# A graph kernel on one core: the first normalisation's root moved from ScalarE to GpSimd and VectorE, six tiles of x in flight, a coarser edge search, and a new order of encoder and adjacency steps

## The reference

```python
h = relu(layernorm(x))                      # x: 1250 nodes x 1024
h = sigmoid(h @ wenc.T + benc)              # 1250 x 500
h2 = h @ conv_weight
agg = segment_sum(h2[src] * edge_weight[:, None], dst)    # 20000 edges, sorted by dst
x = x + (agg + h @ lin_weight.T) @ wdec.T + bdec
h = relu(layernorm(x))
h = h @ W.T + b
# with self loops: out[row] = sum over edges of deg[row]**-0.5 * deg[col]**-0.5 * h[col]
x = x + out
```

## Time and profile before

| | us |
|---|---|
| median of three runs | 539.5 |
| the profiled execution's own time | 540.06 |
| span of the profile | 537.9 |
| TensorE multiplies, busy | 493.9 (92%) |
| VectorE busy | 268.1 (50%) |
| ScalarE busy | 182.8 (34%) |
| GpSimd busy | 30.3 (6%) |
| mean granted TensorE clock | 0.978 |

### The profile page before, as it was taken

The page is one execution under the profiler, slowest core; times in us unless marked ns, Lnnn a source line. Parts: engine busy times, 40 slices in busy tenths (PEclk is TensorE's granted clock), DMA queues, the critical chain, the costliest instruction groups (busy, mean ns, idle before and its releaser), DMA issues.

```text
span 537.9 us, 9411 instructions
## 1 busy us (share of the span) xinstructions
PE 493.9 (92%) x3716; PEld 425.6 (79%) x3716; DVE 268.1 (50%) x663; ACT 182.8 (34%) x348; POOL 30.3 (6%) x27
## 2 busy tenths in 40 slices
PE   3468398899999999999999999999999999999997
PEld 3357397799887877878988887888888888888975
DVE  4587587777768488452456778651111111211211
ACT  0753577855445111211433454550120120120110
POOL 1200000000000000000000000011021030030030
PEclk9977799999999999999999999899999999999999
DMA  8302031155411004006443000700100101100102
GB/s 309 98 11 93 25 118 51 57 175 201 136 66 50 12 0 192 0 2 216 186 151 122 0 2 16 299 1 39 40 1 39 41 1 40 40 1 39 40 1 71
DMA packets 16462, 40.11 MB, mean 75 GB/s; under 512 B 1984, under 2 KB 10442, under 8 KB 16034
## 3 DMA queue, kind: packets, MB, share of 16 engines
q1 hardware_dynamic: 16098, 39.09, 20.2%
q0 software_dynamic: 320, 0.39, 0.2%
HBM read 27.95 MB, written 11.52 MB: 73 GB/s over the span
## 4 chain that ended last, share of the span: by engine, by line
PE 86%; ACT 6%; DVE 6%; issue 1%; POOL 0%; ACTq 0%; DVEq 0%; POOLq 0%
PE bank L1043 21%; PE bank L1044 20%; PE bank L1045 20%; PE bank L1059 16%; PE bank L1163 3%; PE bank L1148 2%; ACT h L598 2%; DVE stats L747 1%; PE bank L1253 1%; PE bank L1150 1%; PE bank L1152 1%; DVE we L431 1%; PE bank L1123 1%; DVE before L771 1%; ACT L608 1%
## 5 line engine op out<-in xcount | busy, mean ns | idle before, releaser
L1059 PE MATMUL bank<-a,h_hi 128*128 128x256 f16 (+3 forms) x400 | 87.5, 273 | 0.0
L1059 PE MATMUL bank<-a,h_lo 128*128 128x256 f16 (+3 forms) x400 | 87.4, 272 | 0.0
L1043 PE MATMUL bank<-w_hi,z 128*128 128x512 f32 (+1 forms) x160 | 62.7, 392 | 1.1 <-DVE z L1018 1.1
L1028 DVE SCALAR_TENSOR_TENSOR x<-bank,dis_u,x 128x512 f32<-128x512 f32 (+1 forms) x20 | 14.9, 750 | 95.2 <-PE bank L1045 95.2
L1044 PE MATMUL bank<-w_lo,z 128*128 128x512 f32 (+1 forms) x160 | 62.4, 390 | 0.0
L1045 PE MATMUL bank<-w_hi,z 128*128 128x512 f32 (+1 forms) x160 | 62.3, 389 | 0.0
L718 ACT CAST z<-bank 128x256 fp32r<-128x256 f32 (+1 forms) x40 | 14.4, 371 | 129.3 <-PE bank L1059 129.3
L589 POOL TENSOR_TENSOR x<-x,bt 128x1024 f32<-128x1024 f32 (+1 forms) x10 | 24.0, 2398 | 477.4 <-ACT bt L726 477.4
L1043 PE MATMUL bank<-h0T,we 128*128 128x256 f32 (+3 forms) x160 | 48.0, 300 | 2.1 <-DVE we L431 2.1
L1044 PE MATMUL bank<-h0T,we 128*128 128x256 f32 (+3 forms) x160 | 46.2, 289 | 0.0
L1045 PE MATMUL bank<-h0T,we 128*128 128x256 f32 (+3 forms) x160 | 46.0, 288 | 0.0
(11 more groups left out here) (140 smaller groups left out, 1072.5 us busy)
## 6 DMA issues: line engine op xcount, KB each, us to landing
adj_scratch<-stage SPq DMA_DIRECT2D x50, 125.0 KB, 1.8
raw<-adj_scratch SPq DMA_DIRECT2D x2, 2500.0 KB, 9.3
h<-x SPq DMA_DIRECT2D x9, 512.0 KB, 4.3
x<-x SPq DMA_DIRECT2D x9, 512.0 KB, 5.2
out<-x SPq DMA_DIRECT2D x9, 512.0 KB
w_raw<-w SPq DMA_DIRECT2D x4, 1024.0 KB, 9.1
wd_raw<-wdec SPq DMA_DIRECT2D x1, 2048.0 KB, 7.8
we_raw<-wenc SPq DMA_DIRECT2D x1, 2000.0 KB, 9.5
```

The lines of the kernel that those rows point to most:

```text
L1028: v.scalar_tensor_tensor(xs, bank[banks_of[g]][0:n, :], dis_u[0:n, t:t + 1], xs, ALU.mult, ALU.add).then_inc(bank_free, 1)
L1043: pe.matmul(o, lhs[0], rhs[0], start=first, stop=False, skip_group_check=True)
L1059: ins = pe.matmul(o, h1[i][0:n, k, 128 * f:128 * (f + 1)], moving, start=(k == 0 and part == 0 and i == 0), stop=(k == T - 1 and part == p ...
```

## The change

1. **The root.** `roots` for the first norm becomes `scale`: VectorE adds epsilon, GpSimd raises to the power -0.5 (one TENSOR_TENSOR of 128x2), VectorE makes a Newton step (three instructions) and the bias, for two tiles together. ScalarE does no square root in the first layer. The second norm keeps its root on ScalarE.
2. **Six tiles.** `XRING` is 6, and all six are loaded at the start; the encoder weight arrives in two halves between them, and the encoder bias last.
3. **The search** looks at every sixteenth destination: 10 comparisons and 20 multiplies. `starts` is a step of its own between `stats 0` and `stats 1`. GpSimd clears the two bias rows and fills two more small tiles ahead of the gather.
4. **The order.** `edges` comes after block 1's transposes and after all of block 0's encoder. In blocks 1 to 3, two encoder groups come before the next block's transposes and two after. `swl 0` is four steps with windows between them.
5. **The windows.** The three multiplies of `hot` are one of 750 elements (line 850), and ScalarE makes all four widened copies (660).

```diff
-ALIGN = 8
+ALIGN = 16
-XRING = 4
+XRING = 6
-    steps = statistics(0, 2) + norms(0) + turn(0) + [("lo", *s) for s in turn(0)] + cut_we + statistics(2, 4)
-    dense = encoder(0)[:2] + norms(1) + [("edges",)] + turn(1) + encoder(0)[2:] + statistics(4, 6) + norms(2) + turn(2)
-    dense += mix(encoder(1), statistics(6, 8) + norms(3)) + turn(3) + mix(encoder(2), statistics(8, 10) + norms(4)) + turn(4)
-    dense += [("load", "wc")] + encoder(3) + cut_wc + encoder(4) + [("load", "wl")]
-    dense += [("g", t) for t in range(5)] + mix(cut_wl, [("g", t) for t in range(5, T)])
-
-    cost = {"t": 0.8, "e": 2.5, "g": 2.6}
+    steps = [("stats", 0), ("starts",), ("stats", 1), ("scale", 0, 2)] + norms(0) + turn(0) + [("lo", *s) for s in turn(0)] + cut_we
+    dense = encoder(0)[:2] + statistics(2, 4) + norms(1) + encoder(0)[2:] + turn(1) + [("edges",)]
+    for b in range(1, NB - 1):
+        dense += mix(statistics(2 * b + 2, 2 * b + 4) + norms(b + 1), encoder(b)[:2]) + turn(b + 1)
+        if b == NB - 2:
+            dense += [("load", "wc")]
+        dense += encoder(b)[2:]
+    dense += mix(encoder(NB - 1), cut_wc) + [("load", "wl")]
+    dense += [("g", t) for t in range(5)] + mix(cut_wl, [("g", t) for t in range(5, T)]) + [("swl", 0, f) for f in range(KF)]
+    cost = {"e": 1.1, "g": 2.0, "swl": 1.5}
-    begin = dense.index(("t", 1, KD // 2 - 1)) + 1
+    begin = dense.index(("edges",)) + 1
...
+            nc.gpsimd.memset(hT[0][96:128, KF - 1, :].bitcast(F32), 1.0).then_inc(bias_rows, 1)
+            nc.gpsimd.memset(hT[1][96:128, KF - 1, :].bitcast(F32), 0.0).then_inc(bias_rows, 1)
...
+                if s[0] == "scale":
+                    t0, t1 = s[1:]
+                    pool.wait_ge(var_ready, t0 // 2 + 1)
+                    nc.gpsimd.tensor_tensor(std[:, t0:t1], dis[:, t0:t1], minus_half[:, 0:t1 - t0], ALU.pow).then_inc(power_ready, 1)
...
+                    y, q, var = std[:, t0:t1], dsq[:, t0:t1], dis[:, t0:t1]
+                    v.tensor_scalar(var, mv[:, t0:t1, 1], EPS, None, ALU.add).then_inc(var_ready, 1)
+                    dve.wait_ge(power_ready, t0 // 2 + 1)
+                    link(v.scalar_tensor_tensor(q, y, -0.5, y, ALU.mult, ALU.mult))
+                    link(v.tensor_tensor(q, q, var, ALU.mult))
+                    link(v.scalar_tensor_tensor(rstd[:, t0:t1], q, 1.5, y, ALU.add, ALU.mult))
+                    v.scalar_tensor_tensor(nbias[:, t0:t1], mv[:, t0:t1, 0], -1.0, rstd[:, t0:t1], ALU.mult, ALU.mult).then_inc(rstd_ready, 1)
...
+                    shape = [128, SUB, WPARTS, KC // 2, 2]
+                    v.tensor_tensor(o_key[:, r, :, 1:, :].rearrange("p w n (c i) -> p w n c i", i=2), key.unsqueeze(2).broadcast_to(shape),
+                                    wq[:, ws, :, :].unsqueeze(3).broadcast_to(shape), ALU.mult).then_inc(pair_ready, 1)
```

More of the change, by code:

```diff
@@ L83, in statistics @@
     def statistics(a, b):
-        return [("stats", t) for t in range(a, b)] + [("roots", a, b)]
+        return [("stats", t) for t in range(a, b)] + [("scale", a, b)]
     def norms(b):
@@ L136, in schedule @@
     turned = [("c", t, q) for t in range(T) for q in range(len(QS))]
-    steps += [("swl", 0), ("general",)]
+    steps += [("general",)]
     for n in range(NS):
         if n:
-            steps += [("swl", n)]
+            steps += [("swl", n, f) for f in range(KF)]
         units = [("unit", n, k) for k in range(T)]
@@ L202, in build @@
         if s[0] == "swl":
-            for f in range(KF):
-                bank_for(("s", s[1], f), *dense)
+            bank_for(("s", s[1], s[2]), *dense)
         elif s[0] == "c":
@@ L271, in build @@
         cb = small("cb", [P, T], F32)
+        minus_half = small("minus_half", [P, 2], F32)
         epsc = small("epsc", [P, 1], F32)
@@ L300, in build @@
         we = [at(f"we{i}", [P, KD, F], F32R, R_G + 16000 * i) for i in range(2)]
-        h0 = at("h0", [P, XRING, D], F32, R_X)
+        h0 = [at(f"h0_{i}", [P, D], F32, R_X + 4096 * i if i < 4 else R_G + 32768 + 4096 * (i - 4)) for i in range(XRING)]
         edges = at("edges", [EP, RG, 3, ROW], I32, R_RAW)
@@ L352, in build @@
         x_in = [sem(f"x_in{t}") for t in range(T)]
-        cut_in = {n: sem(f"{n}_in") for n in ("we", "wc", "wl", "wd")}
+        cut_in = {n: sem(f"{n}_in") for n in ("wc", "wl", "wd")}
+        we_in = [sem(f"we_in{i}") for i in range(2)]
         w1_in = [sem(f"w1_in{i}") for i in range(W1_LOADS)]
@@ L592, in _ @@
         def _(act):
+            act.wait_ge(iotas, 11)
             for s in STEPS:
@@ L772, in _ @@
             ins.then_inc(before_ready, 1)
-            dve.wait_ge(starts_acc, 1)
-            link(v.tensor_scalar(start_f[:], wbank[1][0:EP, 2 * ROWS + 2:2 * ROWS + 2 + RG], -1.0, 0.0, ALU.add, ALU.max))
-            v.tensor_copy(start[:], start_f[:]).then_inc(starts_ready, 1)
             for s in STEPS:
@@ L781, in _ @@
                     dve.wait_ge(x_in[t], 16)
-                    statistics(t, h0[0:n, t % XRING, :], t, n)
-                elif s[0] == "norm":
-                    norm(s[1], 0)
+                    statistics(t, h0[t % XRING][0:n, :], t, n)
+                elif s[0] == "starts":
+                    dve.wait_ge(starts_acc, 1)
+                    link(v.tensor_scalar(start_f[:], wbank[1][0:EP, 2 * ROWS + 2:2 * ROWS + 2 + RG], -1.0, 0.0, ALU.add, ALU.max))
+                    v.tensor_copy(start[:], start_f[:]).then_inc(starts_ready, 1)
+                elif s[0] == "scale":
+                    t0, t1 = s[1:]
+                    dve.wait_ge(mv_ready, t1)
+                    y, q, var = std[:, t0:t1], dsq[:, t0:t1], dis[:, t0:t1]
[5 more added lines that the diff above has]
+                    v.scalar_tensor_tensor(nbias[:, t0:t1], mv[:, t0:t1, 0], -1.0, rstd[:, t0:t1], ALU.mult, ALU.mult).then_inc(rstd_ready, 1)
                 elif s[0] == "cut":
@@ L999, in _ @@
                 elif s[0] == "norm1":
-                    norm(s[1], 1)
+                    norm1(s[1])
                 elif s[0] == "h1lo":
```

101 lines of the change are left out of this document (45 added, 56 removed).

## The result

The changed kernel takes **548.2 us** (median of four runs, 546.87 to 549.55) against 539.5 (four runs beside them): the ratio is 1.015, with a 95% interval of 1.0108 to 1.0192. It is slower, and outside the range of the prediction.

The account below looks back on a forecast made before the run. TensorE bounds the kernel, with 38.5 us idle, all in the first 110 us. Idle time +2.8 (41.3 against 38.5) and work -5.0 make -2.2; 540.06-2.2-0.56 gives 537.3 us, range 534.0 to 541.8.

Parts of the forecast that it names:

- Search: Start: halved comparisons and multiplies take 2.2 us of TensorE work and 2.0 us of idle time away.
- I cost them at nothing: Start: GpSimd's two clearings (1.13 us each) beside VectorE's comparisons cost nothing, at most 2.2 us.
- rival D: Start: clearings hold VectorE's comparisons, the search ends 2.2 us later, 539.1 us in all; chance 0.12.
- The norm starts at 13.6: First norm: starts at 13.6 us against 16.99 before, so block 0's transposes start 3.3 us earlier.
- rival C: Blocks 0 and 2 to 4: GpSimd's power is slow, at 2.4 us the kernel takes 543.9 us; chance 0.10.
- The waits: TensorE's idle times up to the first `sk`, listed place by place: 41.3 us in all against 38.5 before.
- the core of the prediction: Gaps of 2 to 3 us ahead of `e 2 0` and `e 3 0`, which the trace before does not have.
- After so short an idle stretch the transposes run at full speed: Block 2's transposes: behind 2.6 us idle they take 2.2 us instead of 3.5, so -1.3 us of work.
- Rival B: `e 0 0` and `e 1 0`: TensorE is not slowed there, -3.2 us more, 534.1 us; chance 0.36.
- Rival E: Late windows: VectorE falls behind as the fused multiply costs 0.2 to 0.3 us more, +5, 542.3 us; chance 0.05.

Follow-up runs that it names:

- Experiment 1: Changed kernel with the two clearings moved behind the gather and the first power: 547.54 us, ratio 1.0132 to the kernel before.
- 7: Old order with the changed parts, first power ahead of the gather, clearings behind both, one-column sigmoid first on ScalarE: 535.96 us, ratio 0.9888.
- 9: Changed kernel with fields as own step, low parts first, last two `swl 0` groups behind windows, start of 7, next block's norms ahead of `e b 1`: 521.0 us.
- Experiment 2: Changed kernel with the old order of steps, old cost table and `swl 0` whole behind the last window: 540.77 us, ratio 1.0001.
- 11: Kernel before the change with filling multiplies in TensorE's waits: 534.72 us, ratio 0.9907.
- experiment 3: Changed kernel with filling multiplies of the identity in TensorE's waits, no wait shortened: 542.74 us, ratio 1.0045 to the kernel before.
- experiment 10: Kernel of 9 with filling multiplies ahead of the transposes of blocks 2 to 4 and the first window: 520.6 us, ratio 0.9628.

## Why the prediction was wrong

Forecast was -2.2 us for the profiled execution and +9.3 came, 11.5 more. By its own steps:

**Search: right.** TensorE's 4.4 us became 2.3. The wait ahead of it was to be 5.2 and is 7.1, which belongs to the next two points.

**"I cost them at nothing" (the clearings): wrong, rival D.** It gave D a chance of 0.12, and cited as support for zero that small steps beside a clearing kept their 0.16 us. The step that failed is that these say nothing of a 128x128 `tensor_scalar`. The clearings held the three identities ahead of the comparisons, not the comparisons as D had it, for 1.8 us. Experiment 1 shows it: with the clearings moved, the comparisons and all behind them up to block 0's transposes came 1.8 us earlier, and nothing else ahead of these moved.

**"The norm starts at 13.6": wrong by 3.1.** 1.8 are the clearings. The gather began 1.07 us behind the start numbers (9.60 + 0.17 to 10.84), not 0.3; experiment 1 has 1.08 with the clearings out of the way, so they are not the reason, and no run shows what is. (With the power ahead of it, in 7 and 9, the gather starts 0.24 us behind the power.) The power took 0.72 us for 0.4 (rival C's far end did not come). The table load stayed, as forecast. The price against the forecast is 3.0 us of idle time (1.9 ahead of the search, 1.1 ahead of block 0).

**The waits: right nearly everywhere.** Forecast and measured: fields 5.2 and 5.47, first window 3.5 and 3.36, block 2's transposes 2.6 and 2.23, `e 2 0` and `e 3 0` 2.7 and 2.80, block 3's and block 4's transposes 2.2 and 2.23, `e 4 0` 1.2 and 1.34, ahead of `sk` 2.5 and 2.59. Only the windows that wait for a copy cost 1.3 and not 0.5. The two new gaps that were called the core of the prediction are there.

**"After so short an idle stretch the transposes run at full speed": wrong, and the largest miss.** The step took one row, block 3's transposes behind 2.53 us, as a rule for all waits of that length, although its own rows had the opposite as well: `e 0 2` at 0.50 behind a wait of 2.60 us. It counted -2.8 us of busy time, +4.5 came, 7.3 us apart. The single terms, from the first multiply of a step to the next step: block 1's transposes did run at full speed (3.67 to 1.91 us, -1.8 for the -1.5 that was counted). Block 2's kept nearly all of their time (3.15 to 3.04, -0.1 for -1.3). Block 3's (1.81 to 3.27), `e 2 0` (2.95 to 4.44) and `e 3 0` (2.92 to 4.40), which the forecast had at full speed without a word, cost 1.5 us each.

Not all of the 4.5 is the clock. With filling, TensorE's own multiplies ahead of the first `sk` take 9.0 us less in the changed kernel (148.2 to 139.3) and 5.6 less in the kernel before (145.8 to 140.2). So 3.3 of the 4.5 is half speed, 6.1 from the forecast. The other 1.2 remain at full speed. They are mostly in the windows: one that stands ahead of a wait is shown with 0.66 us and another with 0.50, and there are more waits.

Rival B leaned on the same rule from the other side ("since only one idle stretch before block 2 is now over 5 us behind dense work") and fell with it. Its price for `e 1 0` was that of `e 0 2`: before, `e 1 0` ran at full speed (2.96 us).

**Rival E fell.** The fused multiply takes less than the three. From one window's operands to the next VectorE needs 1.06 us in after; before it needed 1.20 (44.75 to 45.94), with 0.68 for the three:

```profile
48.87 0.27 DVE L844 TENSOR_TENSOR o_key<-iota_k,kkey 128x250 bf16<-128x250 bf16 x1
49.07 0.47 DVE L846 TENSOR_TENSOR o_src<-iota_s,skey 128x640 bf16<-128x640 bf16 x1
49.47 0.53 DVE L850 TENSOR_TENSOR o_key<-o_key,wq 128x750 bf16<-128x750 bf16 x1
49.93 0.27 DVE L844 TENSOR_TENSOR o_key<-iota_k,kkey 128x250 bf16<-128x250 bf16 x1
```

Together: 3.0 for the start, 6.1 for the clock, 1.2 for the other busy time, 0.8 for the copies, and 0.4 that I can't assign make the 11.5. This is the sum as the forecast wrote it, busy and idle time apart. It is not what the clock costs net: at full speed TensorE comes earlier to the next wait and waits longer there. Net, half speed costs 5.5 us in the change and 6.0 before, nearly the same.

**Why the new order loses at all** is a second question, since the forecast had it even. Experiment 2 puts it at 7.4 us (8.0), 11 at 8.0 (7.5) with the clock held. The traces of 3 and 11 allow a count of everything ahead of the first `sk` that is not the kernel's own TensorE work, with filling multiplies counted as waiting: 40.5 us in the old order, 49.0 in the new one. Block 2's transposes gain 4.9 (9.0 to 4.1), and those of blocks 3 and 4 gain 0.6 together; `e 2 0` and `e 3 0` lose 2.9 each, and what follows block 4's transposes 6.3 (1.34 ahead of `e 4 0`, 2.4 for windows that wait for a copy, one of them 1.47, and 2.59 ahead of `sk`), where before there was nothing. With the fields and the first window (-0.1) that is +6.5; 1.9 more are the longer wait ahead of block 0 (9.76 against 7.82), which is only the 2.1 us by which the search is shorter. The forecast had the same list: block 2 -5.8, `e 2 0` and `e 3 0` +5.4, behind block 4 +4.2 (1.2, 2.5 and 0.5), +3.8 in all, since the small ones cancel. So the order was forecast as a loss, and then 2.8 us of clock, and what the start should bring, were set against it. Against that +3.8 stand the +6.5 with the clock held: block 2 gains 0.9 less, since the 2.6 us forecast there hold only while `e 1 0` is slow, and what lies behind block 4, the copies above all, costs 2.1 more; the differences elsewhere nearly cancel.

Left open: what decides whether a wait of this length is followed by half speed. In the change block 3's transposes ran at half speed and block 4's at full speed, behind the same 2.23 us; in experiment 1 it was the other way round; and the first `sk` stood behind 2.59 us in the change (1.00) and in experiment 3 (0.50 in 188.2 to 191.4). So the length of the wait alone does not decide it, and no run was made for the rest.

## What to carry to other kernels

A wait on TensorE has a second price, the half speed behind it, and it must be looked up for each place and not from one lucky row: filling the waits with useless multiplies shows in one run how much that price is, and whether it is on the path. When an order moves waits around, work out each new wait at the clock that goes with it, and then look at who makes the engine wait (here late fields, low parts and norms: a few lines of the list moved them, and with the start and half of `swl 0` they took the kernel from 548.2 to 521.0 us). What a filled run gives back is a net price: where the next step waits for a norm anyway, full speed only lengthens that wait, as in experiment 10. A scheduler that spreads work by a cost table answers every edit with other places for everything else, so an edit of 2.6 us may give 7 or nothing.

## What the runs showed of the hardware

- **GpSimd can hold VectorE for a whole instruction.** A `tensor_scalar` of 128x128 beside a clearing of 32x1250 took 1.10 to 1.24 us instead of 0.28. The Trainium skill ("SBUF — State Buffer", Who interferes with whom) has this rule, and this trace agrees: the held time is the clearing's.
- **A power on GpSimd costs 0.69 to 0.73 us for two elements for each partition**, over four times a small VectorE step (0.16).
- **The gather's start** took 1.07 us behind its numbers in the change and 0.33 before.
- **Half speed followed waits of only 2.2 to 3.4 us** at five places of the change, and full speed two such waits (2.23 and 2.59 us); in experiment 1 waits of 2.75 and 2.23 us were followed by full speed, and another of 2.23 by half. The mean clock of one kernel's runs differs as well (0.966 to 0.978 in experiment 1, with 545.35 to 550.47 us), so the slow stretches are not the same in each run.
- **ScalarE's table load** (1.28 us) waits with the instruction that needs it; with a one-column instruction ahead it ran at 0.73 us, off the path.
